# Context pieces to GpSimd, turned tiles first, and reordered fills in a post-norm decoder layer

## What is computed

```python
x = layernorm(x + self_attention(x))          # 32 heads of 16, causal, biases on q, k, v and out
x = layernorm(x + cross_attention(x, ctx))    # 32 query heads of 128, 8 key/value heads, rotary q and k, softmax
x = layernorm(x + ffn(x))                     # 4-bit weights dequantised by groups of 128; silu(x@Wg) * (x@Wu) @ Wd, 1376 wide
```

## Time and profile before

| | |
|---|---|
| time, median of 3 runs | 888.88 us (887.12 to 889.69) |
| the profiled execution's own time | 887.8 us |
| its span | 885.9 us |
| TensorE busy | 841.4 us (95%) |
| VectorE busy | 726.9 us (82%) |
| ScalarE busy | 497.2 us (56%) |
| GpSimd busy | 590.0 us (67%) |

### The profile page before, as it was taken

The page is one execution under the profiler, slowest core; times in us unless marked ns, Lnnn a source line. Parts: engine busy times, 40 slices in busy tenths (PEclk is TensorE's granted clock), DMA queues, the critical chain, the costliest instruction groups (busy, mean ns, idle before and its releaser), DMA issues.

```text
span 885.9 us, 17326 instructions
## 1 busy us (share of the span) xinstructions
PE 841.4 (95%) x6141; PEld 470.2 (53%) x6141; DVE 726.9 (82%) x1129; ACT 497.2 (56%) x1487; POOL 590.0 (67%) x522
## 2 busy tenths in 40 slices
PE   8898999889799999999999999999999899999897
PEld 4666777555445555555555555554555544333343
DVE  5589998877777888879788788798899764899887
ACT  5787889443555555556565565654654652777400
POOL 1264449886647775776677677578788642887885
PEclk9999999999999999999999999999999999999999
DMA  6765245203134413314224215113622412330011
GB/s 181 232 202 161 73 132 163 66 1 120 25 90 126 107 36 85 86 46 132 61 37 120 61 36 153 38 25 87 141 74 41 101 31 71 96 129 3 1 48 47
DMA packets 119893, 76.75 MB, mean 87 GB/s; under 512 B 72861, under 2 KB 104064, under 8 KB 119808
## 3 DMA queue, kind: packets, MB, share of 16 engines
q1 hardware_dynamic: 117504, 74.99, 31.3%
q10 hardware_dynamic: 2304, 0.66, 0.3%
HBM read 52.50 MB, written 6.36 MB: 66 GB/s over the span
## 4 chain that ended last, share of the span: by engine, by line
PE 51%; POOL 15%; DVE 14%; issue 7%; ACT 7%; DMA 4%; SPq 0%; ACTq 0%; DVEq 0%; POOLq 0%
PE bank L359 14%; PE bank L360 14%; PE bank L361 14%; POOL rot L630 3%; DVE total L1305 2%; DMA pT<-pn 2%; POOL pn L647 2%; POOL q2l L636 2%; ACT prob L807 1%; ACT prob L946 1%; DVE rsin L1169 1%; POOL deq L659 1%; DVE nmax L1090 1%; POOL left L663 1%; PE bank L1545 1%
## 5 line engine op out<-in xcount | busy, mean ns | idle before, releaser
L640 POOL TENSOR_TENSOR prob<-prob,rden 128x512 f32<-128x512 f32 x64 | 66.7, 1041 | 124.6 <-DVE rden L1234 124.6
L630 POOL TENSOR_TENSOR rot<-rcos,rsin 128x512 f32<-128x512 f32 x80 | 106.6, 1332 | 19.4 <-DVE rsin L1169 19.3
L359 PE MATMUL bank<-aTh,xqh 128*128 128x512 f16 x256 | 97.0, 379 | 3.5 <-DVE aTl L1059 2.4
L359 PE MATMUL bank<-xoh,o2h 128*128 128x512 f16 x256 | 97.5, 381 | 0.0
L360 PE MATMUL bank<-xol,o2h 128*128 128x512 f16 x256 | 97.3, 380 | 0.0
L361 PE MATMUL bank<-xoh,o2l 128*128 128x512 f16 x256 | 97.3, 380 | 0.0
L361 PE MATMUL bank<-aTh,xql 128*128 128x512 f16 x256 | 97.0, 379 | 0.0
L360 PE MATMUL bank<-aTl,xqh 128*128 128x512 f16 x256 | 97.0, 379 | 0.0
L946 ACT ACTIVATE prob<-bank,ebias 128x128 f32<-128x128 f32 x256 | 90.6, 366 | 2.1
L1169 DVE SCALAR_TENSOR_TENSOR rsin<-bank,sinq 64x512 f32<-64x512 f32 x128 | 88.1, 688 | 1.7
L636 POOL TENSOR_TENSOR q2l<-rot,q2h 128x512 f16<-128x512 f32 x64 | 82.2, 1284 | 4.4 <-ACT q2h L843 4.4
(11 more groups left out here) (212 smaller groups left out, 2626.9 us busy)
## 6 DMA issues: line engine op xcount, KB each, us to landing
tst<-tables SPq DMA_DIRECT2D x11, 768.0 KB, 6.1
xqs<-in_xwq SPq DMA_DIRECT2D x8, 1024.0 KB, 7.2
xos<-in_xwo SPq DMA_DIRECT2D x8, 1024.0 KB, 5.5
qst<-in_fq SPq DMA_DIRECT2D x11, 384.0 KB, 3.4
kstk<-stack SPq DMA_DIRECT2D x48, 64.0 KB, 2.3
qstk<-stack SPq DMA_DIRECT2D x21, 128.0 KB, 2.6
xs<-in_ctxT SPq DMA_DIRECT2D x2, 1024.0 KB, 7.7
res<-in_x SPq DMA_DIRECT2D x1, 2048.0 KB, 8.2
```

The lines of the kernel that those rows point to most:

```text
L359: pe.matmul(out_ap, ah, bh, start=first, stop=False)
L630: nc.gpsimd.tensor_tensor(rot[:, r % 2, :], rcos[:, r % 2, :], rsin[:, r % 2, :], ALU.add).then_inc(rope_rot, 1)
L640: nc.gpsimd.tensor_tensor(prob[:, v % 2, :].rearrange("p (h k) -> p h k", h=QH), prob[:, v % 2, :].rearrange("p (h k) -> p h k", h=QH), rd ...
```

## The change

1. **Context pieces.** The four pieces of half 0 move from VectorE (steps 25, 27, 31, 33) to GpSimd (steps 25, 27, 29, 31), where they are done by `split_piece` with the context's exponent. Two pieces of half 1 stay on VectorE and move from steps 15 and 17 to 25 and 29.
2. **Turned tiles first.** In the self-attention's loop a "t" fill that is first in its step is consumed by ScalarE ahead of the step's exponentials and by VectorE behind the row maximum, ahead of `p1_lo` (steps 55 to 58).
3. **Fills at the start of the cross-attention.** "k" of block 2 goes from the last fill of step T0 + 3 to the first of T0 + 2.
4. **Fills at its end.** "v" of the last block goes from step END - 4 to END - 5, and the "t" fill of batch 0 from END - 6 to END - 5, where that of batch 1 stands already; those of batches 2 and 3 stay at END - 4 and END - 3.
5. **Early gate and up.** `merge` goes ahead of `weigh` in step END + 1, and the gate of tile 2 ahead of the last merge.
6. **Banks of the down products.** `down` writes banks 4 and 5 and waits for the woven products' use of them; `down_codes` takes banks 6 and 7 in place of 4 and 5 and waits there for f_total[0].

```diff
@@ -71,13 +71,13 @@
     plan += [(T0, "o", (4,)), (T0, "o", (5,)), (T0 + 1, "o", (6,)), (T0 + 1, "o", (7,))]
-    plan += [(T0 + 2, "t", (0, 4)), (T0 + 2, "t", (0, 5)), (T0 + 3, "t", (0, 6)), (T0 + 3, "t", (0, 7)), (T0 + 3, "k", (2,))]
+    plan += [(T0 + 2, "k", (2,)), (T0 + 2, "t", (0, 4)), (T0 + 2, "t", (0, 5)), (T0 + 3, "t", (0, 6)), (T0 + 3, "t", (0, 7))]
         plan += [(s, "q", (block, 0)), (s, "k", (block,)), (s + 1, "q", (block, 1)), (s + 2, "q", (block, 2)),
-                 (s + 3, "q", (block, 3)), (s + 3 if block < len(ORDER) - 1 else s + 5, "v", (block,))]
-    plan += [(END - 6 + b, "t", (1, b)) for b in range(4)]
+                 (s + 3, "q", (block, 3)), (s + 3 if block < len(ORDER) - 1 else s + 4, "v", (block,))]
+    plan += [(END - 5, "t", (1, 0)), (END - 5, "t", (1, 1)), (END - 4, "t", (1, 2)), (END - 3, "t", (1, 3))]
@@ -143,7 +143,9 @@
 X_SLOT = {0: 10, 1: 12, 2: 14, 3: 15}
-CTX_SLOT = {(1, 0): 9, (1, 1): 11, (1, 2): 15, (1, 3): 17, (0, 0): 25, (0, 1): 27, (0, 2): 31, (0, 3): 33}
+CTX_SLOT = {(1, 0): 9, (1, 1): 11, (1, 2): 25, (1, 3): 29}
+
+POOL_CTX_SLOT = {(0, 0): 25, (0, 1): 27, (0, 2): 29, (0, 3): 31}
@@ -184,7 +186,7 @@
-EARLY_GU = {END - 2: [0], END: [1], END + 2: [2], END + 4: [3]}
+EARLY_GU = {END - 2: 0, END: 1, END + 2: 2, END + 4: 3}
@@ -380,7 +382,7 @@
         def part_bank(use):
-            return bank[(0, 1, 4, 5, 2, 3)[use % 6]]
+            return bank[(0, 1, 6, 7, 2, 3)[use % 6]]
@@ -581,10 +583,10 @@
-            def split_piece(hi, lo, src, lo_done):
+            def split_piece(hi, lo, src, lo_done, e=E_W):
                 pieces_done += 1
-                nc.gpsimd.tensor_scalar(src, src, 2.0 ** E_W, None, ALU.mult).then_inc(piece_scaled, 1)
+                nc.gpsimd.tensor_scalar(src, src, 2.0 ** e, None, ALU.mult).then_inc(piece_scaled, 1)
@@ -609,7 +611,15 @@
+            def ctx_piece(half, k):
+                cols = slice(half * HALF, (half + 1) * HALF)
+                pool.wait_ge(ctx_in[half], 16)
+                split_piece(cTh[:, k, cols], cTl[:, k, cols], xs[half][:, k, :], cT_lo, E_X)
+
             def pieces(t):
+                for (half, k), slot in POOL_CTX_SLOT.items():
+                    if slot == t:
+                        ctx_piece(half, k)
@@ -912,6 +922,7 @@
                     v1_out(j + 1)
+                bank_splits(turned_first(t))
@@ -933,7 +944,7 @@
                 weight_pieces(t)
-                bank_splits(fills_at(t))
+                bank_splits([f for f in fills_at(t) if f not in turned_first(t)])
@@ -1350,6 +1361,8 @@
                     v1_split_lo(j + 1)
+                for f in turned_first(t):
+                    consume(f)
@@ -1377,7 +1390,8 @@
                 for f in fills_at(t):
-                    consume(f)
+                    if f not in turned_first(t):
+                        consume(f)
@@ -1448,7 +1462,7 @@
                 dve.wait_ge(f_parts, b + 1)
-                nc.vector.scalar_tensor_tensor(out=yh[:, b % 2, :], in0=bank[6 + b % 2][:, :], scalar=2.0 ** (-E_I - E_W),
+                nc.vector.scalar_tensor_tensor(out=yh[:, b % 2, :], in0=bank[WOVEN_BANK[b % 2]][:, :], scalar=2.0 ** (-E_I - E_W),
@@ -1676,19 +1690,19 @@
-            def gate_up(n):
+            def gate_or_up(n, m):
...
@@ -1743,7 +1757,7 @@
                     elif use < 4:
-                        pe.wait_ge((w_gated, w_inter)[use - 2], len(WOVEN))
+                        pe.wait_ge(f_total[0], 2 * len(CODED) - 3 + use)
@@ -1758,7 +1772,7 @@
                 if b < 2:
-                    pe.wait_ge(f_total[0], 2 * len(CODED))
+                    pe.wait_ge((w_gated, w_inter)[b], len(WOVEN))
@@ -1766,7 +1780,7 @@
                         down_codes(b + 1)
-                    last = split_products(pe_, bank[6 + b % 2][:, :], inh[k][:, b * S:(b + 1) * S], inl[k][:, b * S:(b + 1) * S],
+                    last = split_products(pe_, bank[WOVEN_BANK[b % 2]][:, :], inh[k][:, b * S:(b + 1) * S], inl[k][:, b * S:(b + 1) * S],
@@ -1802,16 +1816,22 @@
                     fill(f)
+                if v == STEPS + 1:
+                    merge(v - 3)
+                if v == STEPS + 2:
+                    gate_or_up(EARLY_GU[t], 0)
                     fill(f)
-                if 3 <= v <= STEPS + 2:
+                if 3 <= v <= STEPS + 2 and v != STEPS + 1:
                     late_turn(LATE_TURN[t])
-                for n in EARLY_GU.get(t, ()):
-                    gate_up(n)
+                if t in EARLY_GU:
+                    if v != STEPS + 2:
+                        gate_or_up(EARLY_GU[t], 0)
+                    gate_or_up(EARLY_GU[t], 1)
```

More of the change, by code:

```diff
@@ L1677, in merge @@
                 last.then_inc(c_wo, 1)
-            def gate_up(n):
+            def gate_or_up(n, m):
                 i, half = GATE_UP[n]
-                cols = slice(half * HALF, (half + 1) * HALF)
-                pe.wait_ge(f_wlo, i + 1)
-                if n == 0:
-                    pe.wait_ge(fill_free, NF)
-                if n == 1:
-                    pe.wait_ge(c_exp, STEPS)
-                if n in (2, 3):
-                    pe.wait_ge(f_inter, n - 1)
-                for m, done in ((0, f_gate), (1, f_up)):
-                    project(bank[2 * (n % 2) + m][:, :], [wgh[i][:, m, k * P:(k + 1) * P] for k in range(NK)],
-                            [wgl[i][:, m, k * P:(k + 1) * P] for k in range(NK)], aTh, aTl, cols).then_inc(done, 1)
+                if m == 0:
+                    pe.wait_ge(f_wlo, i + 1)
+                    if n == 0:
+                        pe.wait_ge(fill_free, NF)
+                    if n == 1:
+                        pe.wait_ge(c_exp, STEPS)
+                    if n in (2, 3):
+                        pe.wait_ge(f_inter, n - 1)
+                project(bank[2 * (n % 2) + m][:, :], [wgh[i][:, m, k * P:(k + 1) * P] for k in range(NK)],
+                        [wgl[i][:, m, k * P:(k + 1) * P] for k in range(NK)], aTh, aTl,
+                        slice(half * HALF, (half + 1) * HALF)).then_inc((f_gate, f_up)[m], 1)
             def bank_free(c, p):
```

## The result

The changed kernel takes **884.42 us** (median of 5 runs, 883.54 to 885.03) beside 888.88 before (the median of three runs, and of five); the ratio is 0.9947, 95% interval 0.9935 to 0.9959. It is faster by 4.5 us where 10 were forecast. Its profiled execution takes 884.3 us, 3.5 under that of before.

What follows compares the result with a forecast made beforehand. TensorE, busy 95% of the span, was taken as the bound, with VectorE full in steps 8 to 32. Terms -2.6 - 3.9 - 1.1 - 1.0 - 0 - 1.4 = -10.0 gave 878.3 us, range 874.0 to 883.0.

Steps and rivals of the forecast that it cites:

- Part 1: Self-attention's first half, context pieces: 3.1 us won, 0.5 lost in the third block; net -2.6, from -5.1 to +0.3.
- Part 2: Self-attention's last steps, turned tiles first: waits at the turns and first "q" shrink; net -3.9, bounds -4.5 and -1.9.
- what is late next: Steps 56 to 58: the work itself limits next; a step falls from 5.20 to about 4.6 us, two bring 1.4.
- Part 3: Cross-attention's start: "k" covers the first wait, a late aTl gives back 1.6 us; net -1.1, bounds -4.4 and +1.6.
- Part 4: Cross-attention's end: "v" fills the first wait, a turn then waits for v2l; -1.0 us, bounds 0 and -5.0.
- Part 5: Steps END + 1 and END + 2: no TensorE wait lies there, so 0, give or take 0.5 us.
- Part 6: Ahead of the down products: wait of 1.84 us goes, first codes wait 0.4; net -1.4, from -1.84 to -0.9.
- The engines do hold each other up: Rival: GpSimd blocks VectorE's two returning pieces, 3.3 us each, 2 us more in sum; 881 us, chance 0.15.
- GpSimd's pace: Rival: GpSimd, 4.71 of 5.20 us, sets the pace of steps 56 to 59; part 2 brings 1.9, 880.3; chance 0.10.
- the waits only move: Rival: gains are waited for again at the cross-attention's start; 885 to 889 us, no measurable change; chance 0.08.
- Both low stretches: Rival: both low-clock stretches, at the cross-attention's start and end, go; 3.4 us more won, 874.9; chance 0.10.
- GpSimd's pieces: Rival: GpSimd's context pieces delay step 40's scores; slower, 891 us or more, from 7.0 us a piece; chance 0.04.

Runs made afterwards that it cites:

- two edits on one such chain: Changed kernel with two output-weight pieces off GpSimd, 883.39 us; with exponentials of T0 ahead of q2h, 882.59; with both plus v2h and v2l first, 876.76.

## Why the prediction was wrong

- **What bounds the kernel** was right. A gain ahead of 250 us arrives whole at 690: the lead is 6.36 us at step 76 and 6.45 at END - 6.
- **Part 1** (-2.6) was right, -2.5: 3.0 won and 0.4 lost for 3.1 and 0.5. The two blocks that make up the 3.1 were put at 1.3 and 1.8 and brought 2.0 and 0.95, so that their sum is so near has luck in it. The price of 2.33 us a returning piece was too high; they took 2.01 and 1.40.
- **Part 2** (-3.9) came to -4.4 at the turns and -2.6 at T0 + 2. The waits went as walked. The step that failed is "what is late next": I looked for it in the steps of the turns themselves, where GpSimd did not hold, and not behind them, where GpSimd's weight pieces and four rotations in a row do not move when VectorE and TensorE come earlier. No row of that stretch had been read.
- **Part 3** (-1.1) was right in size: -0.8, with the wait of 2.79 as walked. The late aTl ahead of the next "q" was put at 1.6 us given back, and that wait measured 0.73.
- **Part 4** (-1.0) is the step that made the forecast wrong: +3.5 up to step 133. I put the turn's wait at "weigh's o2h and v2h on ScalarE, about 1.4 us" and left out what stands ahead of both in ScalarE's order, a cast that waits for GpSimd, a copy, and the exponentials; it measured 4.09. The low clock lasted 6.8 us in place of 3.4 as well; how much of the loss is the wait's and how much the clock's is not parted exactly, and why the clock stayed low longer is open (last section). The bounds of 0 and -5.0 had no loss in them.
- **Part 5** (0) is +0.6, just past its 0.5: the late turn's res, which no row of before showed a wait for.
- **Part 6** (-1.4) was right, with the 0.44 at the codes.
- With the 0.4 by which the executions differed from the start, these sum to -3.6; the spans differ by 3.7.
- **Rivals.** The engines do hold each other up, but not as priced, 3.3 us a piece. The Trainium skill, SBUF — State Buffer, section "Who interferes with whom", calls the ports that VectorE and GpSimd share an exclusive lock, for which VectorE's two-port modes, and its instructions with two SBUF inputs, contend. The rows agree with a lock for the cast: the one at 88.31 took 1.03 us and ended at 89.34, 0.28 behind GpSimd's adds, which ended at 89.06; the one at 99.42, which only met the last 0.1 us of a GpSimd instruction, took 0.42. They disagree for the remainder, the instruction with two SBUF inputs: the one at 99.87 took 0.98 us and ended at 100.85, inside GpSimd's scaling of 99.50 to 101.19, which took 1.69. In places of these traces where the other engine is idle the two take 0.68 and 1.49. GpSimd's pace was the right engine but at the wrong place. That the waits only move came true for 1.9 of the 7.4 us of lead at step 60, behind which the rest arrived. Both low stretches stayed, and the one at the end doubled. GpSimd's pieces did not stop the scores.
- The range of 874 to 883 held no case in which a moved fill costs. The kernel is faster, which had a chance of 0.88, but by less than half of the forecast 10 us.

## What to carry to other kernels

Before a fill is moved, walk the consumer's engine instruction by instruction from where the result is ready to where the buffer comes free: the wait is everything that stands ahead in that engine's order, not the two instructions that do the work. An earlier place on the consumer's engine can pay as much as another order on TensorE: here v2h ahead of the step's cast took a wait of 4.09 us down to 0.71 with TensorE untouched, for 3.3 us, and the turn moved on TensorE brought 4.0, which the ratios can't tell apart. And where a stretch gains, read the rows behind it for chains over two engines that keep their own pace; two edits on one such chain can bring 3.5 us together where they bring 0.8 and 1.3 alone.
